# Four row tiles transposed by TensorE instead of DMA at the start, start-up loads and vector steps reordered, and a second PSUM bank for the last output products

## The chip, the core and the metric

The kernel runs on one core of a Trainium2 chip. Five engines work side by side, each through its own instruction stream in order: TensorE (PE, with its weight loads as PEld), VectorE (DVE), ScalarE (ACT), GpSimd (POOL) and SyncE (SP), which here only issues DMAs. They meet at semaphores. The metric is the device time of one execution in microseconds, as the median of several runs. 0.2% of it is 4.4 us.

## What is computed

```python
def reference(x, w_qkv, w_out, b_out, w_gate, w_up, w_down):
    xn = layernorm(x)                       # x: 8 batches of 1024 rows of 512
    # attention over windows of 4 rows, every 2 rows, 8 heads, results added up where windows overlap
    qkv = xn @ w_qkv                        # 512 -> 1536
    win = qkv[:, idx]                       # idx: starts 0, 2, 4 ..., 4 rows each
    q, k, v = split(win)
    o = softmax(q k^T * 512 ** -0.5) v
    att = zeros.at[:, idx].add(o @ w_out + b_out)
    # feed-forward, all operands rounded to a 4-bit grid in blocks of 16
    g, u = fp4(xn) @ fp4(w_gate).T, fp4(xn) @ fp4(w_up).T     # 512 -> 1408
    return x + att + fp4(silu(g) * u) @ fp4(w_down).T
```

## The kernel before

Two programs follow each other on every engine: `attention` (to about 836 us) and `feed_forward` (to the end). In both, a float32 operand is split into a float16 high and low part, and every product is made of three float16 products (high by high, high by low, low by high; `three_products`, L977 is its matmul). A product of the projections is 12 matmuls of 128x512.

`attention` takes one batch of 1024 rows after the other, as 8 tiles of 128 rows. Each engine has an order written out by hand: four strings of steps (head, the two halves of the loop body, tail), which `batches` (L116) runs. A step is a letter and a number; `+` after it means the next batch, `'` the one before. The steps that matter here:

- SP: `l` loads a row tile, `k` stores a normalized tile, `t` (`turn_rows`, L402) transposes a tile's high and low parts by DMA into `xt`, `Q` loads a quarter of `w_qkv`, `C` loads `w_out`, `M` loads feed-forward weights for their maxima, `r` loads the residual rows, `s` stores finished rows, `Z` loads prepared weights. The first two tiles are loaded by SP, tiles 2 and 3 and the first two quarters of `w_qkv` by ACT's queue.
- DVE: `t` row statistics (L697, L700), `n` normalization (L786), `Q` maximum of a weight quarter (L654), `W` gain of the weights (L643 and a chain of small steps after TensorE's `M`), `V` low part of a slice of `w_qkv` (L661), `M` maxima of the other weights, `w` transposes attention weights (L755), `d` adds edges, `f` (`finish`, L776) takes an output product out of PSUM.
- ACT: `x` high part of a row tile (L894), `W` high part of a weight slice (L882), `q`/`v` take a projection out of PSUM (L903, L910), `o` takes attended values out (L928), `h` splits them (L934).
- POOL: `r` (`root`, L536) is the inverse root of the variance of four tiles, `l` low part of a row tile (L550), `C` loads constants and issues three DMAs of the bias (L529), `w` spreads attention weights (L564), `o` low part of attended rows (L573), `b` adds the bias to a residual tile (L556).
- PE: `q0` to `q15` and `v0` to `v7` the projections, `s` scores (L1021), `a` attended values (L1038), `p` output products (`project_out`, L1043), `M0` and `M1` spread a maximum over the partitions (L1054), `F` the first feed-forward products.

PSUM has eight banks: `acc[0..2]` for the projections by turns, `prj` for output products, two for `sps` (scores), two for `ops` (attended values). A projection waits for the one three places before it to be taken out; `q0` can be taken out only when all six `V` are done, since its target lies over the raw weights (`qk_out`, L896). All output products use `prj`, so each waits for the one before to be taken out.

Of the kernel before, what the change touches and what calls it, by code (L numbers as in the profile page):

```python
# [9 lines left out]
ACT = mybir.ActivationFunctionType  # L10
F32 = mybir.dt.float32
F16 = mybir.dt.float16
# [3 lines left out]
P = 128  # L16
B, L, C = 8, 1024, 512
# [3 lines left out]
KC = C // P  # L21
FC = FF // P
TPB = L // P
# [78 lines left out]
def at(b, per_batch, k):  # L102

    return (b + 1) * per_batch + (k + 1)
# [8 lines left out]
def batches(engine, head, first, second, tail, do):  # L116

    follow(head, do, 0)
    with engine.Fori(0, LOOP) as b:
        follow(second, do, b)  # L120
        follow(first, do, b + 1)
    follow(tail, do, B - 1)
# [136 lines left out]
def attention(nc, ctx, x, w_qkv, w_out, b_out, w_gate, w_up, w_down, small, ident, part, normed, ready, late, wsc, raw,  # L259
# [3 lines left out]
    def sb(name, shape, dt=F32):  # L263
        return ctx.enter_context(nc.sbuf_tensor(name, shape, dt))

    def sem(name):
        return ctx.enter_context(nc.semaphore(name))
# [8 lines left out]
    xt = space[:, ends[1]:ends[2]].rearrange("p (a k n) -> p a k n", a=2, k=KC)  # L276
# [5 lines left out]
    sc = sb("sc", [P, 20])  # L282
# [7 lines left out]
    xh, qk, v = shared.xh, shared.qk, shared.v  # L290
# [12 lines left out]
    oh = sb("oh", [P, 4, 2, KC, P], F16)  # L303
    res = sb("res", [P, 4, C])
# [6 lines left out]
    eye, ones, diag = sb("eye", [P, P], F16), sb("ones", [P, P]), sb("diag", [P, 2, P])  # L311
# [3 lines left out]

    acc, prj, sps, ops = shared.acc, shared.prj, shared.sps, shared.ops

    w_in, o_in, c_in, b_in = [sem(f"w_in{k}") for k in range(KC)], sem("o_in"), sem("c_in"), sem("b_in")
    w_max, w_all, setup, w_hi, w_ready = sem("w_max"), sem("w_all"), sem("setup"), sem("w_hi"), sem("w_ready")
    wo_hi, wo_ready = sem("wo_hi"), sem("wo_ready")  # L320
# [5 lines left out]
    xn_done, xhi_done, xlo_done = sem("xn_done"), sem("xhi_done"), sem("xlo_done")  # L326
    xt_in = [sem(f"axt_in{i}") for i in range(4)]
    qkv_done, qkv_out, packed = sem("qkv_done"), sem("qkv_out"), sem("packed")
# [7 lines left out]
    proj_done, biased, final = sem("proj_done"), sem("biased"), sem("final")  # L336
# [31 lines left out]
    QKV = 2 * 8 + TPB  # L368
# [20 lines left out]
    def sync(sp):  # L389
# [112 lines left out]
        def first_edge(b, n):  # L502
# [4 lines left out]
                .then_inc(ve_zero, 16)  # L507

        batches(sp,
# [11 lines left out]
    def gpsimd(pool):  # L521
# [78 lines left out]
        for q, n in per_batch.items():  # L600
            pool.sem_inc(q, n)
        pool.wait_ge(half_set, 1)
        batches(pool,
# [9 lines left out]
    def vector(dve):  # L613
# [162 lines left out]
        def finish(b, i):  # L776
            dve.wait_ge(proj_done, at(b, TPB, i))
            dve.wait_ge(biased, at(b, TPB, i))
            dve.scalar_tensor_tensor(res[:, i % 4, :], prj[:, :], sc[:, 5:6], res[:, i % 4, :],  # L779
                                     ALU.mult, ALU.add).then_inc(final, 1)  # L780

        def normalize(b, i):
# [53 lines left out]
        def unit_gains(b, n):  # L836

            dve.wait_ge(m_all, 2)
            for n in range(2):
# [12 lines left out]
            dve.wait_ge(m_step, 9)  # L852

        batches(dve,
# [17 lines left out]
    def scalar(act):  # L872
# [18 lines left out]
        def high_rows(b, i):  # L891
            act.wait_ge(xn_done, at(b, TPB, i))
            act.wait_ge(xt_in[i % 4], 16 * at(b, 2, i // 4 - 1))
            act.activation(xh[:, i % 4, 0, :], xn[:, i % 4, :], ACT.Copy).then_inc(xhi_done, 1)  # L894

        def qk_out(b, n):  # L896
            g, c = divmod(n, 8)
            act.wait_ge(qkv_done, at(b, QKV, q_use(n)))
            act.wait_ge(s_done, at(b, NG, turn[4 * g + 3] // GT - NG))
            act.wait_ge(packed, at(b, 4, 2 * g + 1 - 4))  # L900
            if isinstance(b, int) and b == 0 and n == 0:
                act.wait_ge(w_ready, NQKV // WB)
            act.activation(qk[:, c, g * 512:(g + 1) * 512], acc[q_use(n) % 3][:, :], ACT.Copy,  # L903
                           scale=QKV_GAIN).then_inc(qkv_out, 1)
# [44 lines left out]
        def first_high(b, k):  # L949
            if k == 1:  # L950
# [1 line left out]
            high(act, rows.q, rows.raw[:, k, :], rows.split, k)  # L952

        batches(act,
# [8 lines left out]
                {"x": high_rows, "q": qk_out, "v": v_out, "e": exponential, "o": attended, "h": out_high,  # L963
                 "B": unit_rounder, "H": high_unit, "W": weights_high, "U": out_weights_high,
                 "I": first_rounder, "J": first_high})

    def tensor(pe, gate_up):
# [3 lines left out]
        def three_products(out, pairs):  # L971

            n = 3 * len(pairs)
            at = 0
            for (a_hi, a_lo), (b_hi, b_lo) in pairs:
                for lhsT, rhs in ((a_hi, b_hi), (a_hi, b_lo), (a_lo, b_hi)):
                    last = pe.matmul(out, lhsT, rhs, start=(at == 0), stop=(at == n - 1))  # L977
                    at += 1
            return last

        def project_qk(b, n):
            g, c = divmod(n, 8)
            for q in xt_in:
                pe.wait_ge(q, 16 * at(b, 2, g))
            if isinstance(b, int) and b == 0 and g == 0:
                pe.wait_ge(w_ready, c * P // WB + 1)
            pe.wait_ge(qkv_out, at(b, QKV, q_use(n) - 3))
            cols, tok = slice(c * P, (c + 1) * P), slice(g * 512, (g + 1) * 512)
            three_products(acc[q_use(n) % 3][:, :], [((wq[:, 0, k, cols], wq[:, 1, k, cols]),
                                               (xt[:, 0, k, tok], xt[:, 1, k, tok]))  # L990
                                              for k in range(KC)]).then_inc(qkv_done, 1)
# [50 lines left out]

        def project_out(b, i):  # L1043
            pe.wait_ge(o_lo, at(b, TPB, i))
            pe.wait_ge(final, at(b, TPB, i - 1))
            three_products(prj[:, :], [((oh[:, i % 4, 0, k], oh[:, i % 4, 1, k]),
                                               (wo[:, 0, k], wo[:, 1, k])) for k in range(KC)]).then_inc(proj_done, 1)

        def column_tops(b, n):
# [17 lines left out]
        def first_products(b, n):  # L1067
# [1 line left out]
            gate_up(pe, 0, 0, n)  # L1069

        batches(pe,
# [6 lines left out]
                {"q": project_qk, "v": project_v, "s": scores, "a": attend, "p": project_out, "M": column_tops, "W": out_ready,  # L1078
                 "F": first_products})

    ended = Ended([(q, 16 * at(B - 1, 2, 1)) for q in xt_in],
                  [(s_done, at(B - 1, NG, NG - 1)), (packed, at(B - 1, 4, 3))],
                  [(pv_done, at(B - 1, ATT, ATT - 1)), (ve_in, at(B - 1, 16 * 4 * TPB, 16 * 4 * TPB - 1))],
                  [(qkv_out, at(B - 1, QKV, QKV - 1))], [(masked, at(B - 1, NG, NG - 1))],
                  [(o_out, at(B - 1, ATT, ATT - 1))], [(final, at(B - 1, TPB, TPB - 1))],
                  [(stored[i], 16 * at(0, 2, 0)) for i in range(2)], [(q, 16 * at(B - 1, 2, 1)) for q in stored],
                  [(late_in[n], 16 * sum(c == n for _, _, _, c in LATE)) for n in range(4)])
# [4 lines left out]
def feed_forward(nc, ctx, normed, part, late, wsc, rows, shared, ended, held, out):  # L1092
# [4 lines left out]
    def sem(name):  # L1097
        return ctx.enter_context(nc.semaphore(name))

    xr, xm, xs, xg, xh, xt = rows.raw, rows.rounder, rows.scales, rows.gains, rows.split, rows.turned  # L1100
# [15 lines left out]

    acc = [t[:, :] for t in shared.acc] + [shared.sps[:, 0, :], shared.sps[:, 1, :], shared.ops[:, 0, :]]
    dps = [shared.ops[:, 1, :], shared.prj[:, :]]
    acc_free = [ended.copied, ended.copied + ended.masked, ended.masked + ended.evacuated]

    def await_all(engine, ends):
        for q, count in ends:
# [5 lines left out]
    xt_in = [sem("xt_in0"), sem("xt_in1")]  # L1128
    ht_in = [[sem(f"ht_{part_}{k}") for k in range(2)] for part_ in ("hi", "lo")]
    gu_done, silu_done, h_done = sem("gu_done"), sem("silu_done"), sem("h_done")  # L1130
    down_done, final = sem("down_done"), sem("ffn_final")
# [303 lines left out]
```

## Time and profile before

| | |
|---|---|
| median of three runs | 2214.14 us (2213.77 to 2217.5) |
| profiled execution, own time | 2211.99 us |
| its span (first to last instruction) | 2209.8 us |
| mean granted TensorE clock | 0.998 of full |
| busy share: PE, DVE, POOL, ACT | 97%, 75%, 55%, 30% |
| TensorE is first given a long run of products at | 31.1 us |
| the feed-forward part begins at | 836.3 us |

The profile has a timeline (instructions in order of time, equal ones merged with their count, and the idle time ahead of a row with what ended it), a table of waits, and tables of busy time and granted clock by stretch. A mean clock near 1 and a busy share of 97% say that little time is left outside of TensorE's own work; the rows further down show where it is.

### The profile page before, as it was taken

To read this page: it belongs to the slowest core of one execution; us is meant where nothing else is said; L and a number is where in the kernel's file an instruction comes from. 1 tells how busy PE (TensorE), PEld (TensorE's weight loads), DVE (VectorE), ACT (ScalarE), POOL (GpSimd) and SP (SyncE) were. 2 spreads that over 40 slices of the span, in tenths; PEclk is the share of its full clock that TensorE was granted. 3 is DMA by queue.
4 is the path that set the end of the run, shared out by engine and by line. 5 is a ranking of instruction groups with operands and counts; after the bars stand their busy time and mean duration, and the time that the engine had idled before them with its cause. 6 is when DMAs were issued, how large, how long until landed. Compare 5 with 4: busy or idle time off the path is not lost.

```text
span 2209.8 us, 46872 instructions
## 1 busy us (share of the span) xinstructions
PE 2152.9 (97%) x16712; PEld 1045.1 (47%) x16712; DVE 1663.1 (75%) x3108; ACT 657.1 (30%) x1009; POOL 1219.6 (55%) x877
## 2 busy tenths in 40 slices
PE   4999999999999989999999999999999999999999
PEld 1445454544545444444444444444444444444444
DVE  7777878778687665778778777787787877878774
ACT  3233333333343322222222222222222232222221
POOL 3266767676675544555555555555555555555553
PEclk9999999999999999999999999999999999999999
DMA  9656666585756444333333433333334333343333
GB/s 270 175 124 177 156 148 180 125 198 127 181 151 167 131 137 129 78 90 80 87 83 79 94 75 85 89 81 87 83 77 91 78 87 84 77 92 76 87 74 68
DMA packets 449418, 251.82 MB, mean 114 GB/s; under 512 B 367282, under 2 KB 373938, under 8 KB 449300
## 3 DMA queue, kind: packets, MB, share of 16 engines
q1 hardware_dynamic: 448404, 246.99, 46.0%
q8 instruction: 98, 1.61, 0.3%
q10 hardware_dynamic: 576, 2.10, 0.2%
q0 software_dynamic: 320, 0.97, 0.2%
q14 instruction: 20, 0.16, 0.0%
HBM read 99.01 MB, written 59.77 MB: 72 GB/s over the span
## 4 chain that ended last, share of the span: by engine, by line
PE 89%; DVE 4%; issue 3%; DMA 1%; SPq 1%; POOL 1%; ACT 0%; DVEq 0%; POOLq 0%; ACTq 0%
PE acc L977 19%; PE prj L1345 7%; PE ops L1345 7%; PE prj L977 6%; PE acc L1326 5%; PE acc L1330 5%; PE acc L1327 5%; PE prj L1347 3%; PE ops L1347 3%; PE acc L1328 2%; PE sps L1328 2%; PE sps L1331 2%; PE acc L1331 2%; PE sps L1329 2%; PE acc L1329 2%
## 5 line engine op out<-in xcount | busy, mean ns | idle before, releaser
L977 PE MATMUL acc<-late 128*128 128x512 f16 x2304 | 518.8, 382 | 15.0 <-DMA late<-xh 10.4
L977 PEld LDWEIGHTS acc<-late 128*128 128x128 f16 x2304 | 220.9, 98 | 281.8 <-issue 21.2
L208 POOL TENSOR_TENSOR qk<-qk,xh 128x1408 f32<-128x1408 f32 x64 | 165.7, 2590 | 230.0 <-DVE qk L245 230.0
L1220 DVE SCALAR_TENSOR_TENSOR qk<-acc,row_gains,xh 128x512 f32<-128x512 f32 x64 | 48.0, 751 | 260.4 <-ACT xh L1285 260.4
L203 POOL TENSOR_TENSOR qk<-qk,xh 128x1024 f32<-128x1024 f32 (+1 forms) x128 | 177.5, 1387 | 111.1 <-DVE xh L224 111.1
L213 POOL TENSOR_TENSOR v<-qk,v 128x1408 f16<-128x1408 f32 x64 | 183.1, 2860 | 100.3 <-ACT v L255 100.3
L1345 PE MATMUL prj<-late,qk 128*128 128x512 f16 x704 | 214.6, 379 | 0.7 <-DMA qk<-v 0.7
L1345 PE MATMUL ops<-late,qk 128*128 128x512 f16 x704 | 214.6, 379 | 0.0
L255 ACT ACTIVATE v<-qk 128x1408 f16<-128x1408 f32 x64 | 88.1, 1377 | 367.4 <-POOL qk L208 367.4
L1326 PE MATMUL acc<-late,turned 128*128 128x512 f16 x512 | 194.0, 379 | 0.4 <-DVE qk L1220 0.4
L1330 PE MATMUL acc<-late,turned 128*128 128x512 f16 x512 | 194.0, 379 | 0.0
L1327 PE MATMUL acc<-late,turned 128*128 128x512 f16 x512 | 194.0, 379 | 0.0
L977 PE MATMUL prj<-wo,oh 128*128 128x512 f16 x768 | 177.6, 381 | 6.4 <-DVE res L779 6.4
L250 ACT ACTIVATE qk<-qk 128x1024 f32<-128x1024 f32 (+1 forms) x128 | 101.2, 791 | 228.7 <-POOL qk L203 228.7
L208 POOL TENSOR_TENSOR raw<-raw,scales 128x512 f32<-128x512 f32 x64 | 67.8, 1060 | 140.6 <-DVE raw L245 140.6
L1347 PE MATMUL ops<-late,qk 128*128 128x512 f16 x352 | 133.4, 379 | 0.0
L1347 PE MATMUL prj<-late,qk 128*128 128x512 f16 x352 | 133.4, 379 | 0.0
L550 POOL TENSOR_TENSOR xh<-late,xh 128x512 f16<-128x512 f32 x64 | 79.0, 1244 | 81.6 <-ACT xh L894 71.5
L903 ACT ACTIVATE qk<-acc 128x512 f32<-128x512 f32 x128 | 75.1, 592 | 157.3 <-PE acc L977 157.0
L977 PEld LDWEIGHTS prj<-wo,oh 128*128 128x128 f16 x768 | 73.4, 98 | 96.0 <-issue 8.8
L564 POOL TENSOR_TENSOR pw<-pg,cst 128x512 f32<-128x512 f32 x72 | 94.4, 1320 | 42.2 <-DVE pg L748 38.1
L245 DVE SCALAR_TENSOR_TENSOR qk<-qk 128x1024 f32<-128x1024 f32 (+1 forms) x128 | 114.1, 891 | 4.4
(158 smaller groups left out, 4440.8 us busy)
## 6 DMA issues: line engine op xcount, KB each, us to landing
normed<-late SPq DMA_DIRECT2D x64, 256.0 KB, 2.7
res<-in_L_attn_x SPq DMA_DIRECT2D x64, 256.0 KB, 3.1
attended<-res SPq DMA_DIRECT2D x64, 256.0 KB, 2.6
raw<-normed SPq DMA_DIRECT2D x64, 256.0 KB, 2.7
v<-attended SPq DMA_DIRECT2D x64, 256.0 KB, 2.7
out<-v SPq DMA_DIRECT2D x64, 256.0 KB, 2.0
late<-in_L_attn_x SPq DMA_DIRECT2D x62, 256.0 KB, 3.9
ready<-turned SPq DMA_DIRECT2D x36, 256.0 KB, 2.3
```

The costliest lines, as they stand in the source:

```text
L203: pool.tensor_tensor(blocks(v), blocks(v), spread(s[2]), ALU.mult).then_inc(q["scaled"], 1)
L208: pool.tensor_tensor(blocks(v), blocks(v), spread(s[3]), ALU.mult).then_inc(q["valued"], 1)
L213: pool.tensor_tensor(h[:, 1], v, h[:, 0], ALU.subtract).then_inc(q["low"], 1)
L245: dve.scalar_tensor_tensor(v, m, ROUND_MIN, v, ALU.max, ALU.subtract).then_inc(q["rounded"], 1)
L250: act.activation(m, v, ACT.Abs, scale=ROUND_Y).then_inc(q["rounder"], 1)
L564: pool.tensor_tensor(pw[:, a % 2].rearrange("p h b (g s) -> p h (b g) s", s=SLOTS), pg[:, a % GT].rearrange("p (h s) -> p h s", s=SLOTS).u ...
L977: last = pe.matmul(out, lhsT, rhs, start=(at == 0), stop=(at == n - 1))
L1326: pe.matmul(g, x_hi, g_hi, start=(c == 0), stop=False)
L1327: pe.matmul(g, x_hi, g_lo, start=False, stop=False)
L1330: pe.matmul(g, x_lo, g_hi, start=False, stop=(c == KC - 1))
L1345: last = pe.matmul(dps[k][:, :], ht[:, k, at], w_hi, start=(at == 0), stop=(at == 2 * FC - 1))
L1347: pe.matmul(dps[k][:, :], ht[:, k, at], w_lo, start=False, stop=False)
```

## The change

There are three parts. At the start, TensorE transposes the first four row tiles (`T0` to `T3`, against the identity, eight 128x128 pieces each, into the four banks of `sps` and `ops` read as float16), and ACT copies them out (`y0` to `y3`); the four DMA transposes go. The start-up orders of SP, POOL, DVE change. In the last batch, the output products with an odd number go to the bank `acc[2]`, those with an even number to `prj`; the feed-forward part then waits in addition for the last of them before it uses that bank. In the loop, TensorE makes `v1+` ahead of `a5`.

```diff
+    flip = [bank.bitcast(F16).rearrange("p (a k t) -> p a k t", a=2, k=KC)
+            for bank in (sps[:, 0, :], sps[:, 1, :], ops[:, 0, :], ops[:, 1, :])]
+    flipped = sem("flipped")
+    def out_bank(b, i):
+        return acc[2] if isinstance(b, int) and b == B - 1 and i % 2 else prj
         batches(sp,
-                "l0 l1 l4 l5 k0 Q2 Q3 l6 t0 t1 l7 t2 t3 k1 C0 M0 M1 l0+ t4 k2 l1+ l2+ l3+ l4+ k3 k4 k5 t5 t6 M2 t7 M3 "
+                "l0 l1 Q2 Q3 l4 l5 l6 l7 k0 C0 k1 M0 M1 l0+ t4 k2 l1+ l2+ l3+ l4+ k3 k4 k5 t5 t6 M2 t7 M3 "
         batches(pool,
-                "C0 r0 l0 l1 l2 C1 l3 r1 l4 l5 l6 r0+ l7 W0 l0+ l1+ w0 w1 l2+ w2 l3+ b0",
+                "C0 r0 l0 l1 l2 l3 C1 r1 l4 l5 l6 r0+ l7 W0 l0+ l1+ w0 w1 l2+ w2 l3+ b0",
         def finish(b, i):
-            dve.scalar_tensor_tensor(res[:, i % 4, :], prj[:, :], sc[:, 5:6], res[:, i % 4, :],
+            dve.scalar_tensor_tensor(res[:, i % 4, :], out_bank(b, i)[:, :], sc[:, 5:6], res[:, i % 4, :],
         batches(dve,
-                "Z0 t0 t1 t2 t3 t4 t5 n0 n1 n2 n3 Q0 Q1 Q2 Q3 W0 W1 V0 V1 t6 t7 n4 V2 V3 V4 V5 M0 n5 M1 n6 t0+ n7 t1+ "
+                "Z0 t0 t1 t2 t3 Q0 n0 n1 n2 n3 Q2 Q1 Q3 W0 W1 V0 V1 V2 V3 V4 V5 t4 t5 t6 t7 n4 M0 n5 M1 n6 t0+ n7 t1+ "
+        def rows_turned(b, i):
+            act.wait_ge(flipped, i + 1)
+            act.activation(xt[:, :, :, i * P:(i + 1) * P], flip[i], ACT.Copy).then_inc(xt_in[i], 16)
         batches(act,
-                "x0 x1 x2 x3 W0 W1 W2 W3 W4 W5 x4 q0 q1 q2 q3 x5 x6 q4 q5 x7 q6 q7 v0 v1 v2 v3 U0 q8 q9 q10 e0 q11 "
+                "x0 x1 x2 x3 y0 y1 y2 y3 W0 W1 W2 W3 W4 W5 x4 q0 q1 q2 q3 x5 x6 q4 q5 x7 q6 q7 v0 v1 v2 v3 U0 q8 q9 q10 e0 q11 "
+        def turn_first_rows(b, i):
+            pe.wait_ge(c_in, 32)
+            pe.wait_ge(xlo_done, at(b, TPB, i))
+            for a in range(2):
+                for k in range(KC):
+                    last = pe.transpose(flip[i][:, a, k, :], xh[:, i, a, k * P:(k + 1) * P], eye[:, :])
+            last.then_inc(flipped, 1)
         def project_out(b, i):
             pe.wait_ge(o_lo, at(b, TPB, i))
-            pe.wait_ge(final, at(b, TPB, i - 1))
-            three_products(prj[:, :], [((oh[:, i % 4, 0, k], oh[:, i % 4, 1, k]),
+            if isinstance(b, int) and b == B - 1:
+                pe.wait_ge(final, at(b, TPB, max(i - 2, -1)))
+                if i == 1:
+                    pe.wait_ge(qkv_out, at(b, QKV, QKV - 1))
+            else:
+                pe.wait_ge(final, at(b, TPB, i - 1))
+            three_products(out_bank(b, i)[:, :], [((oh[:, i % 4, 0, k], oh[:, i % 4, 1, k]),
         batches(pe,
-                "M0 q0 q1 q2 q3 q4 q5 q6 q7 v0 v1 v2 M1 s0 v3 q8 q9 q10 q11 q12 q13 q14 q15 v4 v5 s1 a0 M2 v6 v7 a1 "
+                "T0 T1 T2 T3 M0 q0 q1 q2 q3 q4 q5 q6 q7 v0 v1 v2 M1 s0 v3 q8 q9 q10 q11 q12 q13 q14 q15 v4 v5 s1 a0 M2 v6 v7 a1 "
-                "v0+ p0 a5 v1+ s0+ p1 a6 v2+ p2 a7 v3+ q8+ q9+ q10+ q11+ p3 q12+ q13+ p4 a8 q14+ p5 q15+",
+                "v0+ p0 v1+ a5 s0+ p1 a6 v2+ p2 a7 v3+ q8+ q9+ q10+ q11+ p3 q12+ q13+ p4 a8 q14+ p5 q15+",
-    acc_free = [ended.copied, ended.copied + ended.masked, ended.masked + ended.evacuated]
+    acc_free = [ended.copied, ended.copied + ended.masked + ended.projected, ended.masked + ended.evacuated]
```

The tail of TensorE's order, which is unchanged, ends in `... p6' a3 a4 p7' a5 p0 p1 a6 p2 a7 p3 a8 p4 p5 p6 p7 F0 F1 F2`; DVE's in `... f7' u2 z2 f0 d3 w6 f1 d4 w7 w8 f2 d5 f3 d6 d7 f4 f5 f6 f7`; ACT's in `h2 h3 o5 h4 o6 o7 o8 h5 h6 h7`; POOL's in `b3 b4 o5 o6 b5 b6 b7 o7`.

## Rows read from the trace of the kernel before

**Rows 1.** The page: busy time and share of the span, instructions.

```profile
PE 2152.9 (97%) x16712; PEld 1045.1 (47%) x16712; DVE 1663.1 (75%) x3108; ACT 657.1 (30%) x1009; POOL 1219.6 (55%) x877
```

**Rows 2.** TensorE's waits: line waited for, us in total, times, longest.

```profile
PE acc L977 <- DMA late<-xh: 10.4, 3, 8.6
PE prj L977 <- DVE res L779: 6.4, 9, 1.4
```

**Rows 3.** TensorE's timeline, start-up: start, us, what, [idle before <-releaser].

```profile
21.78 0.77 PE L1054 MATMUL prj<-diag,ones 128*128 128x128 f32 x2 [21.78 <-DVE diag L643]
31.13 30.67 PE L977 MATMUL acc<-late 128*128 128x512 f16 x132 [8.58 <-DMA late<-xh]
61.64 0.38 PE L1054 MATMUL prj<-diag,ones 128*128 128x128 f32 x2
...
66.38 23.88 PE L977 MATMUL acc<-late 128*128 128x512 f16 x103 [2.60 <-issue]
```

**Rows 4.** The timeline of all engines, 4 to 40 us.

```profile
7.50 0.69 DVE L697 BATCH_NORM_STATS2 st<-late 128x6 f32<-128x512 f32 x1
...
8.45 0.69 DVE L697 BATCH_NORM_STATS2 st<-late 128x6 f32<-128x512 f32 x1
...
10.36 0.24 POOL L546 TENSOR_SCALAR ln<-ln 128x4 f32<-128x4 f32 x1 [0.19 <-POOL ln L543]
...
11.46 2.75 DVE L786 TENSOR_SCALAR late<-late,mv,ln 128x512 f32<-128x512 f32 x4
...
12.75 3.59 POOL L550 TENSOR_TENSOR xh<-late,xh 128x512 f16<-128x512 f32 x3 [2.15 <-ACT xh L894]
...
14.13 6.92 DVE L654 TENSOR_REDUCE sc<-qk 128x1 f32<-128x1536 f32 x4
...
23.68 6.34 ACT L882 ACTIVATE late<-qk,sc 128x1024 f16<-128x1024 f32 x6 [8.80 <-DVE sc L634]
...
24.86 2.48 DVE L661 SCALAR_TENSOR_TENSOR late<-qk,sc,late 128x1024 f16<-128x1024 f32 x2 [0.83 <-ACT late L882]
...
32.20 0.55 DVE L786 TENSOR_SCALAR late<-late,mv,ln 128x512 f32<-128x512 f32 x1 [2.04 <-POOL ln L546]
...
32.78 0.63 ACT L894 ACTIVATE xh<-late 128x512 f16<-128x512 f32 x1 [2.76 <-DVE late L786]
...
38.54 1.08 ACT L903 ACTIVATE qk<-acc 128x512 f32<-128x512 f32 x2 [5.13 <-PE acc L977]
```

**Rows 5.** DMA issues from 1.6 to 1.9 us: size of each, us to landing.

```profile
qk<-in_L_attn_w_qkv ACTq DMA_DIRECT2D x1, 768.0 KB, 7.1
```

**Rows 6.** Busy time by stretch: PE, PEld, DVE, ACT, POOL, granted clock, DMA.

```profile
66.00:67.00 1.00, 0.62 (x2) 0.28 (x3) 1.00 (x1) 0.00 (x0) 0.00 (x0) 0.50 0.05 18
796.00:798.00 2.00, 0.35 (x11) 0.30 (x10) 1.97 (x3) 0.00 (x0) 1.44 (x2) 1.00 0.42 83
1400.00:2150.00 750.00, 750.00 (x3685) 360.30 (x3683) 581.32 (x1135) 208.41 (x283) 405.03 (x248) 1.00 0.37 83
```

**Rows 7.** The timeline in the loop, at the moved step, fifth of six turns.

```profile
531.63 0.69 PE L1038 MATMUL ops<-pt,v 64*64 64x64 f32 x32
532.26 2.76 PE L977 MATMUL acc<-late 128*128 128x512 f16 x12
...
536.31 0.59 ACT L928 ACTIVATE ot<-ops 128x512 f32<-128x512 f32 x1
```

**Rows 8.** The timeline of the last batch's output products.

```profile
811.41 2.75 PE L977 MATMUL prj<-wo,oh 128*128 128x512 f16 x12 [1.41 <-DVE res L779]
...
814.62 0.69 PE L1038 MATMUL ops<-pt,v 64*64 64x64 f32 x32 [0.46 <-ACT ot L928]
...
826.71 0.37 SPq L442 DMA_DIRECT2D res<-in_L_attn_x  x1
...
829.55 1.27 POOL L556 TENSOR_TENSOR res<-res,bias 128x512 f32<-128x512 f32 x1 [1.25 <-DMA res<-in_L_attn_x]
...
833.69 2.75 PE L977 MATMUL prj<-wo,oh 128*128 128x512 f16 x12 [0.94 <-DVE res L779]
```

More of the change, by code:

```diff
@@ L962, in scalar @@
                 "o5 h4 o6 o7 o8 h5 h6 h7",
-                {"x": high_rows, "q": qk_out, "v": v_out, "e": exponential, "o": attended, "h": out_high,
+                {"x": high_rows, "y": rows_turned, "q": qk_out, "v": v_out, "e": exponential, "o": attended, "h": out_high,
                  "B": unit_rounder, "H": high_unit, "W": weights_high, "U": out_weights_high,
@@ L1071, in tensor @@
         batches(pe,
[1 row of a table removed]
[1 row of a table added]
                 "s2 a2 q0+ q1+ q2+ W0 a3 q3+ q4+ q5+ a4 q6+ q7+",
                 "p6' v4 s1 a0 v5 a1 p7' v6 s2 v7 a2 q0+ q1+ q2+ a3 q3+ q4+ q5+ a4 q6+ q7+",
[1 row of a table removed]
[1 row of a table added]
                 "v0 v1 p0' s0 p1' a5' v2 v3 q8 a6' p2' a7' q9 p3' a8' q10 q11 q12 p4' q13 q14 q15 v4 a0 v5 a1 s1 p5' "
                 "v6 v7 s2 a2 p6' a3 a4 p7' a5 p0 p1 a6 p2 a7 p3 a8 p4 p5 p6 p7 F0 F1 F2",
-                {"q": project_qk, "v": project_v, "s": scores, "a": attend, "p": project_out, "M": column_tops, "W": out_ready,
+                {"q": project_qk, "v": project_v, "s": scores, "a": attend, "p": project_out, "T": turn_first_rows,
+                 "M": column_tops, "W": out_ready,
                  "F": first_products})
```

## The prediction

> **What bounds the kernel now.** I read the page's busy shares first: TensorE is busy for 2152.9 us of 2209.8, 97% [rows 1]. So what the change can bring is in the 57 us in which TensorE does nothing, plus stretches at the low clock. The table of TensorE's waits says where these are [rows 2]: 10.4 us for DMA transposes, 8.6 of them in one wait, and 6.4 us in nine waits for output products being taken out of PSUM. The timeline places the first: TensorE stands until 21.78 (the weight maximum), again for 8.58 us until the transposed rows have landed, and starts its products at 31.13; from there it runs to `M1` at 61.64 without a wait worth a row [rows 3]. Behind the attention part TensorE is full: 750.00 of 750 us [rows 6], so a lead won before 836 us reaches the end of the kernel, and so does a lag.
>
> **Start-up.** The question is what is late next when the DMA transposes (8.58 us of wait) are gone. I follow the chain of small steps through [rows 4] and shift it.
>
> Normalization `n0` starts at 11.46 because two more statistics steps, the second waiting for its tile, come first. POOL's root is done at 10.60 (10.36 + 0.24). Now one `Q` stands ahead of `n0`. Its quarter was issued at 1.7 and landed 7.1 us later, at 8.8 [rows 5]; one `Q` takes 6.92 / 4 = 1.73, so it ends at 10.5 to 10.7, and `n0` starts at 10.7: 0.76 earlier. Three `Q` follow instead of four: another 1.73. So `M0` moves from 21.78 to 19.3, the first ACT weight step from 23.68 to 21.2, the first `V` from 24.86 to 22.4, done at 23.65.
>
> TensorE's transposes and their copies have to fit ahead of that. The low parts leave POOL 1.20 apart (3.59 / 3), the first at 13.2, the fourth at 16.8, since the three bias issues no longer stand before it (that reorder alone costs nothing: the bias is wanted tens of us later). A transpose of 128 columns has no row. From the 128x512 products that start every 0.216 us (30.67 us for 132, less a slow beginning) or 0.43 at the low clock, a quarter is 0.05 to 0.11; the upper end is 0.38, the float32 128x128 matmul at `M0` (0.77 for two [rows 3]). I take 0.11, since the float16 products are of the same type: 0.9 per tile, less than POOL's pace, so `T3` ends at 17.8. ACT's copy of 1024 columns costs what its weight step does, 6.34 / 6 = 1.06; below by nothing: `y3` ends at 18.9, 2.3 us before ACT's first weight step is wanted. Both are hidden; the cover is 1.5 us for `T3` (`M0` waits behind it in TensorE's order) and 2.3 us for `y3`.
>
> TensorE can then begin `q0` at 23.8, 7.3 us earlier. But it doesn't keep that. `q0` to `q2` fill the three banks; `q3` needs `q0` taken out, and in ACT's order that step stands behind `x4`, the high part of tile 4. Before, `x4` was early and the last `V` was what `q0`'s exit waited for (38.54). Now the statistics of tiles 4 to 7 stand behind all six `V`: the `V` run from 22.4 for 6 x 1.24 = 7.4 to 29.8; four pairs of statistics at 0.95 each (7.50 to 8.45) to 33.6; POOL's root and its hand-over 2.04 to 35.6; `n4` and `x4` 1.2 (0.55 + 0.63), `q0`'s exit 0.54, hand-over 0.1: `q3` at 37.5. TensorE finished `q2` at 23.8 + 36 x 0.216 + 2.0 = 33.6, where 2.0 is what the slow beginning costs (30.67 - 132 x 0.216 = 2.2, of which 0.2 is the last one's tail). So a new wait of 3.9 us stands where there was none.
>
> After a pause the granted clock can fall to 0.50, the lower level of 1.2 GHz: it was so behind the pause of 2.60 us at 66, and not behind one of 1.81 us at 797 [rows 6]. The pause at 66 cost about 1.6 us of slow products. With 3.9 us I take the fall as likely. `M1` then comes at 37.5 + 8 x 2.59 + 1.6 = 59.8 instead of 61.64: a gain of 1.8 us; without the fall 3.4.
>
> SP's queue: the two weight loads pass tiles 4 and 5 and the first store, and the transposes `t0` to `t3` are gone, so `w_out`, the first weights for the maxima and the loads behind them are issued earlier; in total the DMA queues move the same bytes less four transposes. The tile-3 store still waits behind `t4`, and with it `n7`, but `t7` is wanted only by `q8`, at 67, and I get it landed by 60. Everything from `v3` on (weight splits, the first scores) hangs on TensorE and moves with it. I cost this part at nothing.
>
> **Loop.** `v1+` ahead of `a5` makes `a5` 2.6 us later and `v1+` 0.6 earlier, six times. In the tightest turn I found, `a5` stands at 531.63 and its exit on ACT at 536.31 [rows 7]; moved, it ends at 531.63 + 2.59 + 0.69 = 534.9, 1.4 us before. TensorE's count of work is the same and nobody is released later. Cost 0, from 0.2 gained to 0.5 lost per turn.
>
> **Last batch.** Output products wait for the one before to leave `prj`: `p1` 1.41 and `p7` 0.94 [rows 8], `p5` and `p6` as `p7`; the rest of the nine waits and 6.4 us [rows 2] are `p0`, which keeps its wait, `p3` and `p4` with 0.3 each, and two small ones in the loop. With two banks:
> - `p1` starts at 809.9, 1.5 earlier, but `a6` behind it waits for ACT, not for TensorE (814.62, idle 0.46). The gain becomes an idle of 2.1 us ahead of `a6`. `p2` and `a7` stand where they were.
> - `p3` and `p4` are freed of their waits, with the hand-over 0.4 each, so `p4` ends 0.75 early; `p5` saves its 0.94 too and starts at about 824.5, when its low part is just made, and `p6` at 827.1.
> - `p7` needs the low part of tile 7. POOL makes it behind the bias step `b7`, which waited for a residual load (829.55), issued at 826.71 behind the store of tile 4. That store waits for `f4`, which moves up by 0.75: load at 826.0, `b7` from 828.8 to 830.1, low part to 831.2, `p7` at 831.2 instead of 833.69.
>
> The gain is 2.5 us. It hangs on no slow stretch behind the 2.1 us idle at `a6`; that would take 1.6 back. The added wait of the second feed-forward group for the last `finish` is over about 4 us before it is reached.
>
> **Sum.** 1.8 + 2.5 = 4.3 us, against the profiled execution's own 2211.99 (span 2209.8 and 2.2 around it): 2207.7. The median shown lies 2.15 higher, at 2214.14, so 2209.8.
>
> **Rivals.**
> - A. No slow stretch at `q3`, or its wait is shorter than 3.4: 3.4 to 4 + 2.5, about 6: 2208.1. For it: the products before the pause are dense, those before the fall at 66 were not. Against: the wait is the longest of all.
> - B. A slow stretch at `a6` in the last batch too: 4.3 - 1.6 = 2.7: 2211.4. The two cases in rows 6 lie on either side of 2.1 us.
> - C. The four quarters of `w_qkv` share the DMA queues, and the first lands not at 8.8 but with the others, near 12.8: `Q0` then holds `n0` by 4 us and the start-up gives nothing: about 2212.
> - D. The wait at `q3` isn't there, and all 7.3 us are kept: 9.8 in all: 2204.3. I see nothing that would let `q0` out before `x4`.
> - E. Transposes are dearer than 0.18 us each. Then `T3` ends after 19 and holds `M0` and with it the weights' whole chain. At the upper row, 0.38: 13.2 + 32 x 0.38 = 25.4, 6.1 us late, so 2209.8 + 6.1 = 2215.9. Against: a 128x512 product is recorded with 0.38 and still starts every 0.216, so a duration is no pace. The Trainium skill ("TensorE: Matmul & The Clock Gate", section "Part 4: PE-mode transpose") gives about 275 ns for one in a kernel's context; an estimate by that page puts the end of `T3` at 22.0, 2.7 late, and the kernel at 2212.5. The trace of before has no transpose to hold it against.
> - F, slower. The delayed `a5` is wanted. DVE's transpose of attention weights two tiles on and ACT's exit wait for it; if TensorE runs further behind them than in the turn of rows 7, all later steps of the turn shift. It decides from 1.4 us; at worst 2.59 x 6 = 15.5 - 4.3 = 11 us slower, with half of it 2217.6.
>
> **How the numbers follow.** Forecast 0.38, A 0.20, B 0.14, C 0.05, D 0.08, E 0.07, F 0.08. The bound of 0.2% (4.4 us, about what a measurement of this kernel can tell from no change) lies at the forecast itself, so I split it evenly: faster 0.19 + 0.20 + 0.08 = 0.47, within 0.19 + 0.14 + 0.05 + 0.07 = 0.45, slower 0.08. The range takes in A, B, C and most of E, with 1 us for the small waits of the loop falling otherwise: 2205.5 to 2215.
>
> **What would show it.** Right: `q0` starts near 23.8; a wait of about 4 us ahead of the fourth product, put down to ACT or to the rows of tile 4, with a clock of 0.50 behind it; `M1` at 59.8; no `p` but the first of the last batch waits for DVE; about 2 us idle ahead of `a6`; the feed-forward part 2.5 us earlier than the start-up lead alone gives. Wrong: the four transposed tiles after 19; no wait at `q3`; an exit of `a5` that directly follows it; new waits of TensorE between 70 and 790.

## The result: slower by 1.35%, and where the time lies in the profile after

The changed kernel takes 2243.16 us (median; 2239.79 to 2244.77), the one before beside it 2213.95: a ratio of 1.0135, with an interval of 1.0121 to 1.0150. Forecast was 2209.8, with a range up to 2215.0. The profiled execution of after has a time of its own of 2243.98 and a span of 2242.2, 32.4 us more than before.

The page, against [rows 1]: span, then busy time of each engine.

```profile
span 2242.2 us, 46937 instructions
...
PE 2173.7 (97%) x16744; PEld 1054.0 (47%) x16744; DVE 1629.8 (73%) x3108; ACT 658.7 (29%) x1013; POOL 1215.4 (54%) x877
```

TensorE is busy for 20.8 us more with 32 matmuls more, so the same work ran more slowly; its idle time rose from 56.9 to 68.5, 11.6 us. To find the place, one compares the stretches between events that both kernels have: `M1`, the first output product in the loop (`p0` of the first batch), the `p0` six turns of the loop later, and the first feed-forward product. Busy time of TensorE by stretch (start:end, length, busy time, count, granted clock, DMA share, GB/s), first before, then after:

```profile
61.64:136.84 75.20, 70.43 (x1007) 0.95 0.47 137
136.84:727.90 591.06, 585.72 (x7501) 1.00 0.64 158
727.90:836.28 108.38, 96.43 (x1354) 0.98 0.51 161
836.28:2209.80 1373.52, 1369.06 (x6721) 1.00 0.37 83
```

```profile
62.21:142.11 79.90, 72.49 (x1007) 0.94 0.46 133
142.11:762.53 620.42, 599.07 (x7502) 0.97 0.60 151
762.53:867.71 105.18, 95.35 (x1353) 0.98 0.50 159
867.71:2242.20 1374.49, 1369.06 (x6721) 1.00 0.37 84
```

The differences are 0.6 up to `M1`, 4.7 in the rest of the head, **29.4 in the six turns**, -3.2 in the stretch that ends the attention part and 1.0 in the feed-forward part: 32.4. Of the 29.4, 16.0 are idle time (21.35 against 5.34) and 13.4 are busy time, at a granted clock of 0.97 instead of 1.00. The loop, which was forecast at nothing, carries the result. TensorE's waits in the whole of after, against [rows 2], show of which kind:

```profile
PE sps L1045 <- issue: 22.1, 10, 3.2
PE sps L1002 <- POOL xh L560: 14.6, 2, 14.3
PE ops L1062 <- issue: 10.2, 7, 2.3
PE acc L992 <- ACT qk L918: 4.6, 1, 4.6
PE acc L992 <- DVE late L671: 3.8, 1, 3.8
PE prj L992 <- DVE res L789: 1.9, 1, 1.9
PE acc L992 <- POOL oh L583: 1.6, 1, 1.6
```

"issue" means that the profile shows nothing that the engine waited for. Before, such waits of scores (`sps`) and attended values (`ops`) were one of 2.3 us and two of 4.0 us in all; here they are 32.3 us in seventeen, 20.9 us in twelve of them inside the six turns, where TensorE has no other wait. No other engine and no DMA is named for these, which speaks against every rival in which a moved step releases somebody late. In the timeline of TensorE they stand at the same place in each turn; this is the third:

```profile
404.75 0.56 PE L1062 MATMUL ops<-pt,v 64*64 64x64 f32 x21
406.65 0.69 PE L1062 MATMUL ops<-pt,v 64*64 64x64 f32 x11 [1.34 <-issue]
407.27 3.97 PE L992 MATMUL acc<-late 128*128 128x512 f16 x12
...
417.08 2.47 PE L1045 MATMUL sps<-qk 64*32 64x32 f32 x173
421.28 0.31 PE L1045 MATMUL sps<-qk 64*32 64x32 f32 x19 [1.73 <-issue]
```

One step is cut in two: 21 matmuls, a pause, 11 more; and further on 173, a pause, 19 more. All six turns are cut at 11 and at 19 matmuls from the step's end, whatever the other engines do at that moment. The product behind the first pause takes 3.97 us instead of 2.76. The granted clock tells why (busy time by stretch, columns as above with all engines between; the clock is the third number from the end):

```profile
407.27:411.17 3.90, 3.90 (x13) 1.38 (x13) 2.84 (x5) 1.63 (x3) 2.53 (x2) 0.68 1.06 262
```

0.68 is a mixture of the levels 0.50 (1.2 GHz) and 1.00 (2.4 GHz). So a pause of 1.1 to 2.7 us in a row of short matmuls costs its own length, and behind some of them a stretch at the low level too.

What always lies a fixed number of instructions into a step is a border in the instruction stream. The page and the table of DMAs have a queue of kind "instruction". In the fourth turn of before (429.87 to 528.95) and the fourth of after (449.80 to 554.67) it reads (packets, MB, share)

```profile
q8 instruction: 12, 0.20, 0.8%
```

in both: 12 transfers a turn of 0.0164 MB each (98 and 1.61 MB in the whole of before). One lies between 418 and 419 in after, ahead of the end of the second pause above at 421.28:

```profile
q8 instruction: 1, 0.02, 7.6%
```

TensorE's instructions are fetched while it runs, piece by piece. The experiments measure how long a piece is.

### The profile page after: what moved, and what is told of

Its sections match the earlier page's. It is cut to its first block, busy times and chain, and to the rows that moved or that the text cites. A ratio compares the mean times of both kernels' runs of the same rounds, so it can differ in the third digit from the quotient of the medians.

```text
span 2242.2 us, 46937 instructions
## 1 busy us (share of the span) xinstructions
PE 2173.7 (97%) x16744; PEld 1054.0 (47%) x16744; DVE 1629.8 (73%) x3108; ACT 658.7 (29%) x1013; POOL 1215.4 (54%) x877
## 4 chain that ended last, share of the span: by engine, by line
PE 93%; DVE 2%; issue 2%; DMA 1%; POOL 0%; ACT 0%; SPq 0%; ACTq 0%; DVEq 0%; POOLq 0%
PE acc L992 23%; PE prj L992 7%; PE prj L1375 7%; PE ops L1375 7%; PE acc L1356 5%; PE acc L1360 5%; PE acc L1357 5%; PE prj L1377 3%; PE ops L1377 3%; PE sps L1045 2%; PE acc L1358 2%; PE sps L1361 2%; PE sps L1359 2%; PE sps L1358 2%; PE acc L1361 2%; PE acc L1359 2%
## 5 line engine op out<-in xcount | busy, mean ns | idle before, releaser
L992 PE MATMUL acc<-late 128*128 128x512 f16 x2304 | 535.5, 391 | 8.4 <-ACT qk L918 4.6
L992 PEld LDWEIGHTS acc<-late 128*128 128x128 f16 x2304 | 225.6, 100 | 288.0 <-issue 39.6
L992 PE MATMUL prj<-wo,oh 128*128 128x512 f16 x720 | 166.2, 381 | 1.9 <-DVE res L789 1.9
L566 POOL TENSOR_TENSOR res<-res,bias 128x512 f32<-128x512 f32 x64 | 84.7, 1325 | 55.2 <-DMA res<-in_L_attn_x 55.2
```

## The experiments

**Theory.** The transposes put 68 instructions into TensorE's stream ahead of the loop (32 matmuls, 32 weight loads, 4 waits). The stream is fetched in blocks of fixed size, so every border moves by 68 against the work. A scores step is 192 matmuls and as many weight loads, 384 instructions that run through in 1.8 us; a projection's product is 24 instructions in 2.6 us. By the theory, a border that falls deep into short instructions finds its block not yet fetched, and one behind a product doesn't. **Rivals:** the swap of `a5` and `v1+` alone; the kind of the added instructions; another engine that is late.

### e1: before, with 68 semaphore instructions ahead of the first step

```diff
+        for _ in range(68):
+            hold(pe, held)
```

`hold` issues one semaphore instruction of TensorE.

> The kernel before with 68 semaphore increments that nobody waits for, put ahead of TensorE's first step, while TensorE has nothing to do (it stands until 21.8 us). 68 is what the four transposed tiles add to TensorE's stream: 32 matmuls, 32 weight loads and four extra waits. Position theory: TensorE's instructions are fetched in blocks of 16 KB, and the slowdown comes from where the block borders fall in the loop, which moves by 68 instructions. Then this kernel is slower by 25 to 35 us, 2240 to 2249, with waits put down to issue in the loop's scores (about 3 us a turn). Rival 1, the swap of v1+ and a5 in the loop: no change, 2214. Rival 2, the earlier start of TensorE against the other engines: no change, 2214.

Measured: 2242.09 us, before 2214.78, ratio 1.0133 (1.0110 to 1.0156). No part of the change is in this kernel, and it has the whole loss. Its waits:

```profile
PE sps L1023 <- issue: 19.8, 10, 2.9
...
PE ops L1040 <- issue: 9.1, 7, 2.6
```

Ten and seven again, as after has. `M1` is at 61.87 (before 61.64), so nothing was lost ahead of it. The six turns take 614.4 us against 591.1.

### e2: after, with the loop in its old order

```diff
-                "v0+ p0 v1+ a5 s0+ p1 a6 v2+ p2 a7 v3+ q8+ q9+ q10+ q11+ p3 q12+ q13+ p4 a8 q14+ p5 q15+",
+                "v0+ p0 a5 v1+ s0+ p1 a6 v2+ p2 a7 v3+ q8+ q9+ q10+ q11+ p3 q12+ q13+ p4 a8 q14+ p5 q15+",
```

> The changed kernel with the loop's order of before (a5 ahead of v1+). Position theory: the swap moves no instruction from s0+ on, so nothing is gained: 2238 to 2246. Swap theory: the loop is as fast as before, about 2210 to 2214. Start theory: no change, 2243.

Measured: 2241.16 us, ratio 1.0129 (1.0094 to 1.0163): inside the interval of after. The waits are `sps` 22.8 us in ten and `ops` 9.1 in eight. Taking the swap back doesn't help where the borders have been moved.

### e3: before, with the swap alone

The reverse of e2's edit, in the kernel before.

> The kernel before with the loop's new order alone (v1+ ahead of a5). Position theory: within 3 us of 2214. Swap theory: about 2240 to 2250. Start theory: 2214.

Measured: 2225.76 us, ratio 1.0059 (1.0036 to 1.0083). By itself the swap costs 11 us by the medians and 13 by the ratio, 13.9 us in the six turns of its profile (604.96 against 591.06). Neither expectation met it: by the theory the swap was to cost nothing, which left out what stands ahead of a border. TensorE's timeline in a turn:

```profile
442.02 0.69 PE L1038 MATMUL ops<-pt,v 64*64 64x64 f32 x32
442.64 1.27 PE L1021 MATMUL sps<-qk 64*32 64x32 f32 x127
446.54 0.76 PE L1021 MATMUL sps<-qk 64*32 64x32 f32 x65 [2.63 <-issue]
447.26 4.44 PE L977 MATMUL prj<-wo,oh 128*128 128x512 f16 x12
```

The swap leaves the borders where they were, and there is one at 65 matmuls from the end of `s0`. With the product `v1+` ahead of `s0` it cost nothing in the six turns of before, and 0.18 us in one of the six of e7 below; with `a5` there, 64 more short instructions stand ahead of it, and the pause is 1.9 to 2.6 us a turn, in the turn shown with a slow product (4.44 us) behind it. So it isn't the delay of `a5` (rival F) that costs: nobody waits for it.

### e4: after, with 188 semaphore instructions ahead of the first step

188 + 68 = 256: by the theory the borders stand as before, if a block has 256 instructions.

```diff
+        for _ in range(188):
+            hold(pe, held)
```

> The changed kernel with 188 semaphore increments ahead of TensorE's first step, so that 68 + 188 = 256 instructions, one block of 16 KB, are added ahead of the loop in all. They run while TensorE stands idle (to 14.3 us). Position theory: the loop has its block borders where the kernel before has them, 98.5 us a turn, and the whole is 2208 to 2214: start-up 0 to 1 us late, last batch about 3.5 us early. Swap or start theory: it stays at 2243.

Measured: 2238.65 us, ratio 1.0122 (1.0103 to 1.0141). The time alone looks like a refutation. Its timeline says what the padding did:

```profile
32.70 1.87 PE L1004 MATMUL sps<-eye,xh 128*128 128x128 f16 x16 [32.70 <-issue]
```

The first transpose starts at 32.70 instead of 14.33: 188 such instructions take up to 0.17 us each, and the start-up lost 14.6 us (`M1` at 76.83 against 62.21). Its waits in the loop are those of e3: scores 15.7 us in seven, six of them in the turns and cut at 65 matmuls from the end; a turn takes 100.6 us, and 100.8 in e3. That is the cost of the swap at the old borders. The time as a test of the block was spoilt by the padding; e5 and e7 use a cheaper one.

### e5: before, with 256 short instructions ahead

64 float32 products of 32 rows by 32 columns, each four instructions, whose result is overwritten.

```diff
+        pe.wait_ge(half_set, 2)
+        for _ in range(64):
+            pe.matmul(prj[0:32, 0:32], ones[0:32, 0:32], ones[0:32, 0:32], start=True, stop=True)
```

> The kernel before with 64 matmuls of 32x32 in float32 (two weight loads and two matmuls each in TensorE's stream, 256 instructions or one block of 16 KB) ahead of its first step, where TensorE stands idle to 21.8 us. Theory of block borders: what counts is the position modulo one block, so the loop runs as before, 98.1 us a turn, and the whole is within 3 us of 2214. Rival: more instructions ahead of the loop are slower as such, whatever their number: 2240 or more, as with 68.

Measured: 2210.07 us, ratio 0.9990 (0.9979 to 1.0000). 256 instructions more cost nothing, while 68 cost 27 us (e1). The timeline shows them, done long before the start-up wants TensorE:

```profile
3.68 7.00 PE L972 MATMUL prj<-ones 32*32 32x32 f32 x128 [3.68 <-issue]
```

### e9, e10, e11: before, with 68, 128 and 192 such instructions

The same edit with 17, 32 and 48 products.

> The kernel before with 68 more TensorE instructions ahead of its first step, this time 17 small float32 products of 32 rows by 32 columns (each is four instructions), whose result is overwritten. Theory of the block borders (instructions are fetched 256 at a time, and a border inside a run of short instructions costs a stall): it depends on the number alone, so as with the 68 semaphore steps of e1: 2238 to 2244 us, turns near 101.7 us, 15 or more waits of scores put down to issue. Rival, that the kind of instruction counts (the semaphore steps themselves, or events they leave behind, made e1 slow): as before within 3 us, 2210 to 2216, since 64 such products cost nothing.

> The kernel before with 128 more instructions (32 such small products), half a block. Theory of the block borders: the time depends on where the borders fall, with a period of 256; half a period away from the kernel before all borders lie elsewhere, so the time differs from before by more than 4 us, more likely slower (5 to 35 us), and it doesn't lie on a line between 0 and 256 (both equal). Rival, that more instructions ahead of the loop cost in proportion to a threshold between 68 and 256 that has nothing to do with blocks: no figure follows from it; it would have to make 128 and 192 like one of their neighbours only.

> The kernel before with 192 more instructions (48 small products), that is 64 short of a whole block. Theory of the block borders: each border falls 64 instructions later in the program's work than in the kernel before, where 68 more had put it 68 earlier; the border that e1 has inside the scores should then lie outside or elsewhere in them: any time from 2210 to 2245, with the stalls counted where the borders lie (each stall in a run of scores or attended values 1 to 3 us and a slow stretch of 1.7 us behind some). Rival of a start-up cause (what lies ahead of M0 costs): the time stays within 3 us of before, since small products ahead of M0 lie in TensorE's first wait.

Measured: 2240.71 us (1.0117, 1.0091 to 1.0143), 2255.28 us (1.0211, 1.0181 to 1.0242) and 2239.82 us (1.0135, 1.0105 to 1.0165). 68 of another kind cost what 68 semaphore instructions do: the number counts, not the kind. The waits of e9 are ten at scores and seven at attended values, as in e1; fifteen at scores had been expected. e10 lies above its expected 5 to 35 us. Over the positions 0, 68, 128, 192 and 256 the time goes 0, +28, +43, +28 and -2 us: it comes back at 256, and there is no slope.

The places of the cuts are the sharper test. One and the same border, early in the attention part, for e9, e10 and e11:

```profile
116.47 0.29 PE L1024 MATMUL sps<-qk 64*32 64x32 f32 x14 [2.08 <-issue]
```

```profile
108.96 0.58 PE L1024 MATMUL sps<-qk 64*32 64x32 f32 x44 [1.85 <-issue]
```

```profile
105.17 0.86 PE L1024 MATMUL sps<-qk 64*32 64x32 f32 x76 [0.60 <-issue]
```

From 68 to 128 instructions the border should fall 60 earlier, which is 30 matmuls with their weight loads: 14 + 30 = 44 matmuls are left behind it. From 128 to 192 it is 64, or 32: 44 + 32 = 76. Both to the matmul. In the loop, e10 is cut with 7 left and e11 with 39 = 7 + 32 (at 300.47 and 299.60). The borders are fixed in the stream, and the work slides over them.

The single transfers of q8 in the traces tie the pauses to the fetches. The one between 418 and 419 in after starts at 418.69 and takes 1.22 us; the pause ends 1.4 us after it has landed. It is so with all 149 pauses put down to "issue" behind 50 us in the thirteen traces: each ends 1.2 to 1.6 us after a transfer of 16,384 bytes has landed. Counted over TensorE's recorded instructions (matmuls, weight loads and those of its sequencer), the 30 of them that lie ahead of the loop all fall at 193 plus a multiple of 256.

They also say how far ahead a block is asked for. At each of after's 17 pauses the transfer had started 0.8 to 2.4 us after TensorE passed the border one block earlier, and the pause ended 3.2 to 4.7 us after that border, while the 256 instructions between had run through in 1.1 to 2.5 us. So what decides is how long the 256 instructions ahead of a border take, more than how many short ones are left behind it. A turn has ten borders. In after's six turns the two that are cut had 1.3 to 2.5 us of work ahead of them, one other had 1.9 and wasn't cut, and the rest had 4.2 us or more. In before's six turns one border a turn had 1.6 us ahead and wasn't cut, and the rest had 2.8 us or more. (The first border behind the loop's branch is left out of this count.)

A long product ahead isn't always enough. e10 also pauses inside `v0+`, the first step of the loop's body, with 4 matmuls of the projection left, for 0.90 to 1.59 us in five turns: there the border comes eight matmuls behind the branch that closes the loop.

### e6: before, with the two banks alone

> The kernel before with the last batch's output products by turns in two banks, and nothing else. In the changed kernel the stretch from the last batch's first output product to the first feed-forward product is 25.5 us and before it is 29.0. Two banks are worth that: 3 to 3.6 us faster, 2210.5. Rival: the stretch is shorter there only because other engines had caught up while TensorE stood in the loop; then 1 to 2.5 us faster.

Measured: 2210.64 us, ratio 0.9996 (0.9986 to 1.0005), which can't be told from nothing. From `p0` of the last batch to the first feed-forward product it takes 833.75 - 807.22 = 26.53 us; before 836.28 - 807.25 = 29.03. That is 2.50 us less, which meets the rival of the expectation (1 to 2.5), and the waits stand where the prediction had them, at `a6` and at `p7`:

```profile
813.48 0.69 PE L1042 MATMUL ops<-pt,v 64*64 64x64 f32 x32 [0.92 <-ACT ot L932]
...
831.15 2.76 PE L981 MATMUL acc<-wo,oh 128*128 128x512 f16 x12 [2.30 <-POOL oh L577]
```

### e7: after, with the old loop order and 188 instructions (47 of the small products)

The start-up and the two banks stay, the borders stand as before.

> The changed kernel with the loop's order of before and 47 float32 matmuls of 32x32 (188 instructions, with the 68 of the transposes one block of 16 KB) ahead of its first step, in TensorE's idle time. Theory that position and swap are the whole of the loop's loss: turns of 98.1 us, start-up 0 to 1 us late, last batch 3 us early: 2210 to 2214. Rival, that the different start of the loop (other engines further behind or ahead) costs as well: 2220 or more.

Measured: 2208.53 us, ratio 0.9984 (0.9975 to 0.9994). With the borders back, and with no useful work taken out, the changed kernel goes from 2241.16 (e2) to 2208.53 us; its six turns take 591.3 us, as before. Start-up:

```profile
24.22 9.83 PE L995 MATMUL acc<-late 128*128 128x512 f16 x36 [3.84 <-DVE late L671]
38.01 22.57 PE L995 MATMUL acc<-late 128*128 128x512 f16 x96 [3.96 <-ACT qk L918]
60.41 0.38 PE L1086 MATMUL prj<-diag,ones 128*128 128x128 f32 x2
```

### e8: e7, with the first exits ahead of the high part of tile 4

```diff
-                "x0 x1 x2 x3 y0 y1 y2 y3 W0 W1 W2 W3 W4 W5 x4 q0 q1 q2 q3 x5 x6 q4 q5 x7 q6 q7 v0 v1 v2 v3 U0 q8 q9 q10 e0 q11 "
+                "x0 x1 x2 x3 y0 y1 y2 y3 W0 W1 W2 W3 W4 W5 q0 q1 q2 x4 q3 x5 x6 q4 q5 x7 q6 q7 v0 v1 v2 v3 U0 q8 q9 q10 e0 q11 "
```

> As the one with 188 instructions and the loop's old order, and in ACT's head the exits of q0, q1 and q2 stand ahead of x4. If TensorE's wait of 4.6 us ahead of q3 comes from x4 in ACT's order alone, and the slow clock behind it (3 us) from the wait, both go: q3 follows q2 with 0 to 0.5 us, and the kernel is 6 to 7.5 us faster than its twin, 2203 to 2207. Rival: the last of the six weight steps holds the exit as long: no change.

Measured: 2204.61 us, ratio 0.9964 (0.9951 to 0.9978): faster than both kernels, and 3.9 us faster than e7, where 6 to 7.5 had been expected. The wait at `q3` is gone:

```profile
24.80 20.82 PE L995 MATMUL acc<-late 128*128 128x512 f16 x84 [3.84 <-DVE late L671]
46.24 10.52 PE L995 MATMUL acc<-late 128*128 128x512 f16 x48 [0.62 <-ACT qk L918]
56.60 0.38 PE L1086 MATMUL prj<-diag,ones 128*128 128x128 f32 x2
...
63.68 4.64 PE L995 MATMUL acc<-late 128*128 128x512 f16 x12 [4.94 <-issue]
```

`M1` is at 56.60, 5.04 earlier than before. Of that, the wait put down to issue at the head's first scores takes back 2.3 (4.94 against the 2.60 in [rows 3]). It is the same kind of border, and it stands in the rows of before. Its transfer started 3.4 us after the border one block earlier, in before 1.0; what held it up isn't known.

## Why the prediction was wrong, step by step

**Loop: "TensorE's count of work is the same and nobody is released later. Cost 0".** This is the step that failed. Both halves of the sentence are true: the twelve new waits in the six turns name no other engine, and the work is the same. What it left out is that TensorE's instructions themselves are delivered; in place of 0 this came to 29.4 us, 20.9 of them pauses at borders (the other waits of the turns shrank by 4.9) and 13.4 slower work. Two parts of the change touch this: 68 instructions ahead of the loop move all borders (e1 and e9, +27 and +28 us with nothing else changed), and the swap puts `a5` and `s0` side by side, 448 short instructions in a row (e3, +11 to 13 us at the old borders; nothing to be told at the new ones, after against e2). The two don't add up, since each decides by where the borders fall. [Rows 3] carry a wait of 2.60 us "issue" ahead of 66.38, and the table that [rows 2] come from has further ones at the scores and the attended values. The prediction used the first for the price of a slow stretch and never asked what it was. In the six turns of before there is no such wait at all; that none of their 60 borders costs anything was luck of position, which no row of before states.

The Trainium skill ("Runtime: NRT & Kernel Launch", section "Instruction fetch mechanics") says that an engine's instructions are refilled in blocks of 16 KiB, 256 instructions, and calls the cost of crossing such a border mostly hidden. The block agrees with the runs: 0.0164 MB a transfer, and the time is back after 256 instructions (e5, e7). That the cost is hidden holds for before's turns; in after the borders cost 20.9 us of pauses in six turns, and here the measurement decides.

**Start-up: gain 1.8 forecast, 0.6 lost in the profiled execution of after (`M1` at 62.21).** The chain was right in kind. Rows of all engines in after, against [rows 4]:

```profile
10.05 1.75 DVE L664 TENSOR_REDUCE sc<-qk 128x1 f32<-128x1536 f32 x1 [1.60 <-DMA qk<-in_L_attn_w_qkv]
...
11.72 2.74 DVE L796 TENSOR_SCALAR late<-late,mv,ln 128x512 f32<-128x512 f32 x4
...
14.33 1.01 PE L1002 MATMUL sps<-eye,xh 128*128 128x128 f16 x8 [14.33 <-POOL xh L560]
```

- `n0` at 10.7: it came at 11.72, since `Q0` waited for its quarter of `w_qkv` until 10.05, not 8.8. That is rival C by 1.2 of its 4 us: the landing isn't the one of [rows 5]. Which of the transfers under way delays it, no run shows. `q0` came at 24.79 instead of 23.8.
- Transposes at 0.11 each, 0.9 a tile: eight take 1.01 us (they start 0.11 apart, and each is recorded with 0.26 to 0.31), ACT's copy 1.02 (forecast 1.06). `T3` ended at 18.9 and `M0` started at 20.18, behind `diag` and not behind `T3`. Rival E is out: the cover was 1.3 us.
- A wait of 3.9 at `q3` until 37.5, put down to ACT: it was 4.55 until 38.57, with `x4` at 37.31.
- The slow stretch at 1.6: it depends on the execution. After had 23.80 us for the 96 matmuls behind it, at a mean granted clock of 0.87 (`M1` at 62.21); e7 22.57 at 0.92 (60.41); e2, whose wait was 3.16, 20.88 at 1.00 (59.28). Against e2 the stretch costs 2.9, 1.7 and 0, and `M1` comes 2.4 and 0.6 later and 0.5 earlier than the forecast 59.8, with the low clock deciding, as rival A had it.
- "D. I see nothing that would let `q0` out before `x4`": one order string does (e8), and it brings 3.8 of the missing us.

**Last batch: 2.5 us.** e6 has 2.50. In e7 and e8 it is 26.78 and 26.61 against 29.03, 2.25 and 2.42, and the idle ahead of `a6` is 2.04 us in both (0.92 in e6), where 2.1 was forecast, with no slow product behind it (2.76 us), so rival B is out. In after itself the stretch shrank by 3.55 (842.23 to 867.71), and `a6` waited 0.67 only; that ACT and POOL had caught up during the loop's pauses is likely, but not shown.

**The range.** With the two terms that were thought through, e7 gives 2208.5, inside it and 1.3 from the forecast. Against before beside it that is a gain of 3.9 us, where 4.3 was forecast; its profile shows 1.2 at `M1` and 2.25 in the last batch. That profile is of its slowest execution (2212.82), in which the borders ahead of the last batch cost 2.52 and 1.73 us and a slow product each behind them (5.30 and 4.41 us), so that the feed-forward part begins 0.9 later than before. The ends of the range had no room for a cost of a kind that no row had been asked about; rival F carried the only ending that is slower by more than 2 us, of up to 11 us and by another mechanism. It is out: nobody waits for `a5`.

**Left open.** A border with 14 matmuls left costs 2.08 us and one with 76 left 0.60 (e9, e11). The 256 instructions ahead took 1.1 and 1.3 us; the difference is that the transfer of the first started 1.0 us after the border one block earlier, that of the second 0.5 us before it. What sets the start of a transfer is open, and so is why the low clock follows some pauses and not others. The median of e10 lies 10.5 us above the lowest of its executions (2244.79, at a mean granted clock of 0.993), which is the one with the profile; the others had 0.987 to 0.991, and where they lost it was not seen.

## What to carry to other kernels

Where TensorE runs hundreds of short instructions in a row, an edit anywhere ahead of them, even one that removes idle time, can move the borders at which its instructions are fetched; a pause put down to "issue" that cuts a step at the same count in every turn is the sign. Test for it with padding: if adding the complement to a whole block (here 256) brings the time back, judge the edit by that kernel, not by the unpadded one. And keep a long product between two steps of short instructions rather than putting them side by side.

## What the runs showed of the hardware

- TensorE's instructions came in transfers of 0.0164 MB, 12 in a turn of 99 us (before) and 12 in one of 105 us (after), and the time of the kernel came back after 256 instructions: 2212, 2241, 2255, 2240 and 2210 us at 0, 68, 128, 192 and 256.
- Each of 149 pauses ended 1.2 to 1.6 us after such a transfer had landed. At after's 17 pauses the transfer started 0.8 to 2.4 us after the border one block earlier was passed, and the block could be run 3.2 to 4.7 us after it.
- The border inside the scores `s0` paused TensorE for 1.9 to 2.6 us with `a5` ahead of them (e3), and for 0 to 0.18 with a product of 2.6 us ahead (before and e7). The longest pause inside scores or attended values was 4.42 us (e2).
- 188 semaphore instructions at the start of TensorE's stream delayed it to 32.7 us, up to 0.17 us each; 256 instructions of small float32 products took 7.0 us, 0.03 each.
